# The norm in front of a small cross attention moved into the feed-forward before it, and its last two norm chains into the causal attention behind it

## What is computed

```python
# L1_attn, last lines: h is the mixer's result, hn its RMS norm
ffn = jax.nn.silu(hn @ wg) * (hn @ wu) @ wd        # 345 inner features
return h + ffn
...
x = _layernorm(x + _L1_attn_ref(...))               # the norm that is moved forward
x = _layernorm(x + _L1_xattn_ref(x, ctx, ctx, ...)) # small cross attention: 16 heads of 8, 32 keys
x = _layernorm(x + _L1_ffn_ref(x, ...))             # begins with h = _rmsnorm(x, ln1_w), causal attention
```

## Time and profile before

| | us |
|---|---|
| median of 3 runs | 1920.94 |
| lowest, highest | 1920.47, 1921.06 |
| profiled execution, its own time | 1921.35 |
| its span in the trace | 1919.5 |
| TensorE busy | 1678.0 (87%) |
| VectorE busy | 1306.9 (68%) |
| ScalarE busy | 955.1 (50%) |
| GpSimd busy | 297.8 (16%) |

### The profile page before, as it was taken

The page is one execution under the profiler, slowest core; times in us unless marked ns, Lnnn a source line. Parts: engine busy times, 40 slices in busy tenths (PEclk is TensorE's granted clock), DMA queues, the critical chain, the costliest instruction groups (busy, mean ns, idle before and its releaser), DMA issues.

```text
span 1919.5 us, 24917 instructions
## 1 busy us (share of the span) xinstructions
PE 1678.0 (87%) x8058; PEld 742.1 (39%) x8058; DVE 1306.9 (68%) x3077; ACT 955.1 (50%) x2057; POOL 297.8 (16%) x460
## 2 busy tenths in 40 slices
PE   6889999999999989999799677446888899979998
PEld 2345544544544422222244221223533454524443
DVE  7477767767767778886663799999455777733333
ACT  2555645646645526667433556333245366643333
POOL 0000000000001022210378000000000222104443
PEclk8999999999999989999999889777798699979999
DMA  4000000000000220230000000000101332000000
GB/s 185 1 1 1 1 1 1 1 1 1 1 1 29 45 73 31 50 106 2 1 1 0 1 1 1 1 1 1 66 0 49 98 74 74 3 1 1 1 0 22
DMA packets 19807, 44.37 MB, mean 23 GB/s; under 512 B 3872, under 2 KB 13024, under 8 KB 18912
## 3 DMA queue, kind: packets, MB, share of 16 engines
q1 hardware_dynamic: 19200, 42.39, 7.5%
q10 hardware_dynamic: 480, 0.39, 0.1%
HBM read 32.74 MB, written 9.44 MB: 22 GB/s over the span
## 4 chain that ended last, share of the span: by engine, by line
PE 72%; DVE 18%; ACT 5%; issue 4%; POOL 1%; DMA 0%; ACTq 0%; POOLq 0%; SPq 0%; DVEq 0%
PE ps L569 8%; PE ps L535 7%; PE ps L547 6%; PE ps L1018 6%; PE ps L968 5%; PE ps L1056 5%; PE ps L504 3%; PE ps L1462 3%; PE ps L1351 3%; PE ps L1463 3%; PE ps L1470 3%; PE ps L1362 3%; DVE arena L1801 2%; PE ps L524 2%; PE ps L578 2%
## 5 line engine op out<-in xcount | busy, mean ns | idle before, releaser
L1173 DVE TENSOR_REDUCE stat<-ps 128x1 f32<-128x512 f32 (+3 forms) x512 | 279.0, 582 | 82.5 <-PE ps L968 41.3
L1104 ACT ACTIVATE arena<-ps 128x512 f32<-128x512 f32 (+3 forms) x512 | 246.6, 515 | 155.6 <-PE ps L1056 81.6
L681 ACT ACTIVATE arena<-ps,stat 128x544 f32<-128x544 f32 x256 | 180.4, 710 | 227.2 <-DVE stat L723 227.2
L723 DVE TENSOR_REDUCE stat<-ps 128x1 f32<-128x544 f32 x256 | 173.6, 720 | 146.8 <-PE ps L535 146.0
L968 PE MATMUL ps<-arena 72*128 72x128 bf16 (+1 forms) x480 | 166.6, 356 | 10.2 <-DVE stat L1173 6.1
L1056 PE MATMUL ps<-arena 75*128 75x512 bf16 (+1 forms) x480 | 164.0, 346 | 9.3 <-ACT arena L1104 7.1
L535 PE MATMUL ps<-arena 64*128 64x272 f32 x1024 | 155.1, 422 | 12.1 <-ACT arena L681 10.4
L569 PE MATMUL ps<-arena 128*64 128x512 f32 (+1 forms) x640 | 159.9, 611 | 6.3 <-DVE arena L743 5.5
L689 ACT COPY arena<-ps 128x512 f32<-128x512 f32 x256 | 137.0, 593 | 14.7 <-PE ps L547 14.7
L547 PEld LDWEIGHTS ps<-wA_sb,arena 128*128 128x128 f32 x1024 | 113.9, 141 | 68.1 <-issue 67.3
L547 PE MATMUL ps<-wA_sb,arena 128*128 128x128 f32 x1024 | 138.5, 279 | 0.0
(11 more groups left out here) (340 smaller groups left out, 2821.3 us busy)
## 6 DMA issues: line engine op xcount, KB each, us to landing
arena<-b_parts SPq DMA_DIRECT2D x180, 96.0 KB
b_parts<-arena SPq DMA_DIRECT2D x64, 128.0 KB, 1.8
reg<-wM_dram SPq DMA_DIRECT2D x1, 3072.0 KB, 10.2
reg<-wB_dram SPq DMA_DIRECT2D x1, 2048.0 KB, 12.6
reg<-wM_dram SPq DMA_DIRECT2D x1, 2048.0 KB, 16.7
reg<-wD_dram SPq DMA_DIRECT2D x1, 1817.0 KB, 10.0
wF_sb<-wF_dram SPq DMA_DIRECT2D x1, 1476.0 KB, 19.8
reg<-b_parts SPq DMA_DIRECT2D x12, 96.0 KB
```

Source lines behind the costliest of these rows:

```text
L681: e.activation(prob_of(P, r).rearrange("p (a k) -> p a k", a=2), score_banks(r), ACT.Exp, bias=x_neg[:, at_:at_ + 1], accum_out=x_sums[:, ...
L723: e.tensor_reduce(x_neg[:, n % 4:n % 4 + 1], score_banks(r), AX.XY, ALU.max, negate=True).then_inc(sem("max_done"), 1)
L1104: e.activation(p_t[:, m % 8, q0:T], ps[:, S1 + m % S2, q0:T], ACT.Exp).then_inc(exp_done, 1)
L1173: e.tensor_reduce(nm[:, G % 2, u // 4, u % 4:u % 4 + 1], ps[:, step % S1, 0:keys(u)], AX.X, ALU.max, negate=True).then_inc(max_done, 1)
```

## The change

1. The norm behind the feed-forward is taken out of `make_norm` and done batch by batch: mean and variance matmuls of batches 0 to 2 (means) and 0 and 1 (variances) stand within the feed-forward (L1979, L1985), the rest in the first units of the cross attention. The table of logarithm and exponential is loaded on ScalarE straight after the last Silu; roots 0 and 1 and the scale of batch 0 follow there. Variances 0 and 1 are first copied out of bank 7 by VectorE (L1995).
2. The queries go to banks 4 and 5 instead of 6, at units 0, 1, 2 and 4. The head-wise keys are laid out a little later.
3. In the loop the norm chains of batches 0 and 1 stand one unit earlier, `total` at the head of a unit, the reciprocal at its tail.
4. In the drain, the projections of batch 1 stand behind the last output projection; VectorE's split of batch 0 is cut in two halves with `total(2)` and `heads(3)` between them.
5. The norm chains of batches 2 and 3 stand in the first 30 steps of the causal attention.

```diff
-                    if border is not None and step == 2:
-                        border["pe_last"](e)
+                    if border is not None:
+                        border["pe"](e, step)
...
+                if b and i == 2:
+                    a_mean(e, b - 1)
+                if b >= 2 and i == 0:
+                    a_var(e, b - 2)
...
+            def b5_context_act(e, b, i):
+                if (b, i) == (B - 1, FC - 1):
+                    e.preload_act_table_set("natural_log_exp_and_others")
+                    a_root(e, 0)
+                    a_root(e, 1)
...
+            def a_mean(e, b):
+                if b == 0:
+                    e.wait_ge(sem("b5_blocks"), 1)
+                e.wait_ge(sem("b4f_sum"), b + 1)
+                if b:
+                    e.wait_ge(bank7_r, a_r + 2 * b - 1)
+                e.matmul(ps[:, 6, :], wt["centre"], x_aux[:, b, :], start=True, stop=True).then_inc(bank7_w, 1)
+
+            def a_var(e, b):
+                e.wait_ge(f_squared, B + b + 1)
+                if b:
+                    e.wait_ge(bank7_r, a_r + 2 * b)
+                e.matmul(ps[:, 7, :], ones, dev[:, b, :], start=True, stop=True).then_inc(bank7_w, 1)
+
+            def a_square(e, b):
+                e.wait_ge(bank7_w, a_w + 2 * b + 1)
+                e.tensor_copy(cent[:, b, :], ps[:, 6, :]).then_inc(bank7_r, 1)
+                e.wait_ge(bank7_r, a_r + 2 * b + 1)
+                e.tensor_tensor(dev[:, b, :], cent[:, b, :], cent[:, b, :], ALU.mult).then_inc(f_squared, 1)
+
+            def a_keep(e, b):
+                e.wait_ge(bank7_w, a_w + 2 * b + 2)
+                e.tensor_copy(dev[:, b, :], ps[:, 7, :]).then_inc(bank7_r, 1)
+
+            def a_root(e, b):
+                if b < 2:
+                    e.wait_ge(bank7_r, a_r + 2 * b + 2)
+                    e.activation(dev[:, b, :], dev[:, b, :], ACT.Ln, bias=v("eps5")).then_inc(a_ln, 1)
+                else:
+                    e.wait_ge(bank7_w, a_w + 2 * b + 2)
+                    e.activation(dev[:, b, :], ps[:, 7, :], ACT.Ln, bias=v("eps5")).then_inc(bank7_r, 1)
+                if b < 2:
+                    e.wait_ge(a_ln, b + 1)
+                else:
+                    e.wait_ge(bank7_r, a_r + 2 * b + 2)
+                e.activation(dev[:, b, :], dev[:, b, :], ACT.Exp, scale=-0.5).then_inc(f_rooted, 1)
+
+            def a_scale(e, b):
+                e.wait_ge(f_rooted, B + b + 1)
+                e.tensor_tensor(x_cur[:, b, :], cent[:, b, :], dev[:, b, :], ALU.mult).then_inc(f_normed, 1)
+            a_ln = sem("b5_inv")
 
...
-                e.wait_ge(*fin5.done(B - 1))
+                e.wait_ge(sem("b5_blocks"), 2)
                 query(0)
-                e.wait_ge(sem("b5_blocks"), 1)
+                a_var(e, 2)
                 e.wait_ge(sem("load_wF"), 16)
-                for n_ in range(N5 + 9):
...
+                    if n_ in QUERY_AT:
+                        query(QUERY_AT.index(n_) + 1)
+                    if n_ == 0:
+                        a_mean(e, 3)
+                    if n_ == 1:
+                        a_var(e, 3)
+                    if n_ in (N5, N5 + 1):
+                        for j in range(2):
+                            border["pe_qk"](e, 0, 2 * (n_ - N5) + j)
+                    for kind, at_ in (("m", 10), ("s", 11), ("t", 13)):
+                        if (n_ - at_) % 4 == 0 and 0 <= (n_ - at_) // 4 < 2:
+                            g_pe(e, kind, (n_ - at_) // 4)
                     if (n_ - 6) % 4 == 0 and 0 <= (n_ - 6) // 4 < B:
                         pv((n_ - 6) // 4)
                     if (n_ - 9) % 4 == 0 and 0 <= (n_ - 9) // 4 < B:
...
-                    if n_ == N5 + 4:
-                        for j in range(4):
-                            border["pe_qk"](e, 1, j)
-                    if n_ == N5 + 6:
-                        border["pe_v"](e)
+                for j in range(4):
+                    border["pe_qk"](e, 1, j)
+                border["pe_v"](e)
 
...
+                a_root(e, 2)
+                for n_ in range(N5 + 4):
+                    if n_ == N5 + 3:
+                        inverse(B - 1)
+                    for step, kind, at_ in ((g_root, "t", 14), (g_square, "s", 11), (g_root, "s", 12), (g_square, "t", 13)):
+                        if (n_ - at_) % 4 == 0 and 0 <= (n_ - at_) // 4 < 2:
                             step(e, kind, (n_ - at_) // 4)
-                    if 2 <= n_ <= B:
...
-                    if n_ == N5 + 2:
-                        border["split"](e, 0, (0, 1))
-                    if n_ in (N5 + 8, N5 + 9):
-                        for j in range(2):
-                            border["dve_qk"](e, 1, 2 * (n_ - N5 - 8) + j)
+                    if (n_ - 8) % 4 == 0 and 0 <= (n_ - 8) // 4 < 3:
+                        heads((n_ - 8) // 4)
+                border["split"](e, 0, (0, 1), (0, 1))
+                total(2)
+                heads(3)
+                border["split"](e, 0, (0, 1), (2, 3))
+                g_scale(e, "t", 1)
+                total(3)
+                for j in range(4):
+                    border["dve_qk"](e, 1, j)
                 border["dve_v"](e)
             pe_steps.append(b5_pe)
             act_steps.append(b5_act)
...
+            CHAIN = {("m", 2): 1, ("s", 2): 6, ("t", 2): 11, ("m", 3): 16, ("s", 3): 21, ("t", 3): 26}
+
+            def chain_pe(e, step):
+                for (kind, b), at_ in CHAIN.items():
+                    if step == at_:
+                        g_pe(e, kind, b)
+
+            def chain_act(e, step):
+                for (kind, b), at_ in CHAIN.items():
+                    if kind != "m" and step == at_ + 1:
+                        g_root(e, kind, b)
+                    if kind != "t" and step == at_ + 3:
+                        g_square(e, "s" if kind == "m" else "t", b)
+
+            def chain_dve(e, step):
+                for (kind, b), at_ in CHAIN.items():
+                    if step == at_ + (1 if kind == "m" else 2):
+                        if kind == "m":
+                            g_centred(e, b)
+                        else:
+                            g_scale(e, kind, b)
+            border.update(pe=chain_pe, act=chain_act, dve=chain_dve, bank7=(bank7_r, r_0 + 3 * B))
             b6_res = narrow(1, x_aux, [g_norms(b)[1] for b in range(B)], x_aux, "b6", "wF", "m_q", "m_k", "m_v", "m_wo",
                             rope=("m_qr", "m_kr"), border=border)
             c = Carve()
```

125 lines of the change are left out of this document (64 added, 61 removed).

## The result

| | before | after |
|---|---|---|
| median, us | 1920.94 (5 runs, 1917.35 to 1921.90) | **1910.84** (5 runs, 1908.55 to 1912.84) |
| profiled execution, its span | 1921.35, 1919.5 | 1912.84, 1911.0 |
| TensorE, VectorE, ScalarE busy | 1678.0, 1306.9, 955.1 | 1671.2, 1307.9, 954.3 |

The ratio of the times is 0.9948, 95% interval 0.9934 to 0.9963: 10.1 us faster, where 11.6 were forecast (1909.3 us). The profiled execution of after is the slowest of its five, so its span shows only 8.5 us.

What follows compares the result with a forecast made beforehand. Feed-forward bound by TensorE, other stretches by chains of waits and the lower clock; 4.3 - 11.6 + 3.5 - 14.4 + 6.6 = -11.6 us, giving 1909.3 us, own range 1906 to 1912.5, with rivals (a) and (b) 1899 to 1916.

Steps and rivals of the forecast that it cites:

- the first query: At the end of the feed-forward: the first query starts 0.6 us behind the last down-projection.
- the two waits of the loop: Cross attention: TensorE idles 2.3 us ahead of batch 3's variance and 2.8 us for batch 0's square on ScalarE.
- the first causal score: End of the drain: the first causal score comes about 18 us earlier than before.
- the clock in the score steps: Score-only steps of the causal attention: granted clock 0.50, the lower level.
- Feed-forward: Five norm matmuls of 0.86 us now stand where TensorE is full: +4.3 us.
- Border: Last down-projection to first reduction: 14.8 to 3.2 us, -11.6, the higher clock level kept.
- Loop: Cross attention, first reduction to last subtraction: 39.9 to 43.4 us, +3.5, from two more matmuls and two new waits.
- rival (b): New gaps cost clock before the score steps: two to four spells, 3 to 6 us, 1912.5 to 1915.5; chance 0.15.
- Drain: Last subtraction to first causal score: 35.4 to 21.0 us, -14.4; lower bound 17, upper 26.
- Score-only: Steps 0 to 31 of the causal attention: 17.9 to 24.5 us, +6.6, at the lower clock level.
- rival (a): Higher clock holds through score steps: 20.5 us there, 5.4 back behind step 32; -21.0, 1900 us; chance 0.24.
- Rival (d): Clock stays low in the loop from the wait for batch 3's variance: up to +25, 1934 us; chance 0.05.

Runs made afterwards that it cites:

- the second execution: The changed kernel profiled again with nothing changed, as a measure of spread: median 1910.5 us, ratio 0.9960 to before.
- variance and reads: Changed kernel with batch 3's variance one unit later and VectorE's reads of batch 0's projections ahead of its scale: 1903.5 us, ratio 0.9922.
- the late chain: Kernel with both edits (variance and reads), plus norm chains of batches 2 and 3 at steps 33 to 60 instead of 1 to 28: 1901.2 us, ratio 0.9903.
- variance later: Changed kernel with batch 3's variance one unit down TensorE's list, behind score 2 and query 2, its root likewise on ScalarE: 1907.4 us, ratio 0.9926.
- the rest alone: Changed kernel with the norm put back behind the feed-forward; loop, drain and causal chains stay changed: 1910.5 us, ratio 0.9955 to before.
- chain late: Changed kernel with the norm chains of batches 2 and 3 at steps 33 to 60 instead of 1 to 28: 1907.4 us, ratio 0.9934.

## Why the prediction was right, and where it was off

The time and the sign held: 1909.3 forecast, 1910.8 measured. So did the mechanism in the main, that is, which matmuls and waits each interval gains and loses. The sizes held less well, and the agreement of the total is partly luck, as the end of this section shows. Of the signs that the forecast named, the first query (0.76 us behind the last down-projection) and the two waits of the loop came. Three numbers didn't: the loop took 46.1 us and not 43, the first causal score came 12.2 us earlier and not 18, and the clock in the score steps was 0.83 and not 0.50. The steps:

1. *Feed-forward.* Forecast +4.3, measured +4.4. Five matmuls at 0.86; no late product. VectorE's busy time there rose from 16.55 to 21.36 us and TensorE stayed at 38.48 of 39.
2. *Border.* Forecast -11.6, measured -10.9. Query 0 starts 0.76 us behind the last down-projection, where 0.6 was said. The rest is mostly the matmuls behind a wait: 0.94 us from the query's start to the next (1412.12, 1413.06) and 1.03 from there to score 0, instead of 0.86 each. The table load takes 1.28 and the activation starts 0.02 us behind it. The drain of 1.38 that the Trainium skill gives (ScalarE: Activation LUTs, "What ACT_TABLE_LOAD costs") isn't in this trace either. By it the query would have started 1.4 us later.
3. *Loop.* Forecast +3.5, measured +6.2; this term was mis-sized. Both new waits are there, with sizes close to those walked out: 2.19 (2.3) and 2.67 (2.8). What failed is the loop's sum, in two terms. The first is the clock: it took 1.0 us off for the level that before lost there (it was low for 1.7 us behind the first reduction, so 0.8) and put nothing in for another loss; one spell at the lower level, behind one or the other wait, costs 1.7. That was rival (b)'s mechanism, below the 3 us of its small end. The second is a matmul: the step counts two more in the loop, but the mean of batch 3 stands behind score 0 (1415.02 in the rows above) and so in the loop too, 0.7 us of it behind the first reduction. TensorE has 161 passes there and had 155, which is three matmuls. All waits together grew by 3.1 us (7.3 against 4.2), where the sum had 2.8. With these, 2.4 of matmuls + 3.1 of waits - 0.8 + 1.7 = 6.4, against 6.2 measured.
4. *Drain.* Forecast -14.4, measured -11.6, and -13.1 in the second execution. Both ways ended close together, as the step said, but both later. The transfers were issued at 1479.46. The step's 4.4 us from there to the score held an estimated landing of 2 us, which no run here shows; in the two kernels whose first score waits for a read-back (variance and reads, with and without the late chain) it was released 5.4 to 5.6 us behind the first issue. By that they would have let after's score go at 1484.9 to 1485.1, and it went at 1485.07. VectorE's way, whose fourth read ended at 1484.9, was as long. The walk had VectorE at 9.1 us behind the last subtraction with the first eight operations; it was 10.0, since the second pair of projections ran at the low level behind the wait of 2.47 (3.50 for four passes). Heads of batch 3 waited 0.93 for their reciprocal, which the walk had ready, and the split ended at 16.0 instead of 14.3. Then the four projections of batch 1 took 6.20 for eight passes, where 3.4 were counted, partly beside VectorE's two operations: 7.8 instead of 6.4. That is 23.8. The step had put the lower clock only into its upper bound of 26; the granted clock was 0.78 from the last subtraction to the first score, and 0.85 in the second execution.
5. *Score-only.* Forecast +6.6, measured +5.6. VectorE's idle time is 5.65 us in the rows above (0.63, 0.22, 1.08, 0.42, 0.94, 2.36), where 5.2 were forecast. The idle time was right and its reason only in part: the level is low in two stretches, not throughout, and about 1.6 us are waits for ScalarE's squares, which the step called hidden. The 15.4 us of maxima were too many: they hold the waits of the lower level. The stretch is 12.8 of maxima + 1.1 ahead of the first + 3.9 of the chain's operations + 5.65 idle = 23.5.
6. *Behind step 32*, not in the sum: 2.9 us gained, and most of it far from the change. At its head the level was low for 8.7 us behind step 32, and 10.8 before. But up to the group of value matmuls shown with the result (L1018 at 1690.04 before, at 1682.56 in after) the column is only 0.8 us shorter. The other 2.0 lie in its last 6 us: before, the level fell once more at 1689.8, within the column (that group takes 1.94 there and 1.06 in after), and in after only at 1691.3, behind it. The forecast had put a gain behind step 32 only into rival (a). In the executions without chains behind step 32 the column goes with the time at the low level in it, from 174.2 us with none to 180.9 with 17 us of it.

Steps 2 to 4 missed by 0.7, 2.7 and 2.8 us, all to one side; 1.0 at step 5 and 2.9 behind step 32 gave most of it back, and the profiled execution is itself 2.0 us above the median. So the agreement within 1.5 us owes something to errors of both signs. Rival (a) was mispriced: with the clock at 0.93 through the score steps they still took 23.0 us, not 20.5, because the waits for squares remain. Its 5.4 behind step 32 came near: in the kernel with variance later and reads first the level was high there throughout, and the column is 6.7 us shorter than before's, 2.0 of it in the last 6 us. Rival (d) didn't happen: no execution of the changed kernel had more than one spell in the loop.

## What to carry to other kernels

Moving work out of a stretch of waits pays what the stretch is long, but put each moved matmul where its operand is ready already: in an engine that works its list in order, a matmul that is two microseconds early holds every score behind it (variance later: 3 us for one matmul and its root, 1.2 of waits and 1.7 of clock). When two waits near 2 to 3 us follow each other, price one spell of the lower clock for them, about 1.7 us here, and don't try to say behind which: in this loop all six executions with waits of 2.2 and 2.5 to 2.7 us had exactly one. Before work is moved into a stretch that another engine bounds, count what it costs in the stretch that it leaves behind, too: 32 steps later the same chains cost 8 to 9 us where they had cost 7 to 8. And look for differences in the clock even where nothing was changed: 1.5 us at the first matmuls of the feed-forward (the rest alone) and 2.0 us at the end of the causal attention were such spells.

## What was not expected of the hardware

- The granted clock's fall isn't a function of the program alone. The same instructions lost the level behind a wait of 2.18 us in one execution (L1985 at 1.95) and behind one of 2.67 us in another (L2098 at 1.62), and not behind the other of the two.
- The low level through score steps bound by VectorE costs little: four maxima came in 1.93 us at 0.50 and in 1.6 at 1.00 (chain late), although a score of 512 columns (L968 in after) takes 0.63 us instead of 0.38.
- A pair of float32 matmuls directly behind a wait takes about 0.95 us to the next start instead of 0.86 (1451.09 to 1452.05, 1412.12 to 1413.06).
